# A graph network with a routed edge stage: the messages in two fp32r parts, a VectorE loop of twelve slots, and three columns of the routing marks on GpSimd

## The reference, cut to what matters

```python
x = x + gnn(layernorm(x), stack([src, dst]), edge_weight1, ...)
x = x + ffn(layernorm(x), ...)

def gnn(h, e, d2, ...):                 # 3125 nodes of 256, 103125 edges
    ei, ej = e[0], e[1]
    msg = silu(concat((h[ei], h[ej], d2)) @ mW1 + mb1)
    msg = layer_norm(msg, ln_g, ln_b)
    msg = silu(msg @ mW2 + mb2)
    agg = segment_sum(msg, ei, num_segments=3125)
    y = silu(concat((h, agg)) @ uW1 + ub1) @ uW2 + ub2
    return h + y
```

## Time and profile before

| | |
|---|---|
| time, median of 3 runs (lowest to highest) | 2228.12 us (2223.9 to 2229.85) |
| the profiled execution: time, span | 2226.9 us, 2225.2 us |
| busy share of the span | PE 88%, DVE 78%, ACT 59%, POOL 56% |
| mean granted TensorE clock | 0.946 |
| instruction packets (queues q8, q14) | 27 and 22 |

### The profile page before, as it was taken

The page is one execution under the profiler, slowest core; times in us unless marked ns, Lnnn a source line. Parts: engine busy times, 40 slices in busy tenths (PEclk is TensorE's granted clock), DMA queues, the critical chain, the costliest instruction groups (busy, mean ns, idle before and its releaser), DMA issues. The chain is left out here.

```text
span 2225.2 us, 45282 instructions
## 1 busy us (share of the span) xinstructions
PE 1961.5 (88%) x11037; PEld 1681.0 (76%) x11038; DVE 1736.7 (78%) x4578; ACT 1303.2 (59%) x2495; POOL 1238.9 (56%) x1177
## 2 busy tenths in 40 slices
PE   3546765379999999999999999999999999799996
PEld 2324554268888888888888888888888888677775
DVE  5899999678877877877878878778778778345895
ACT  1112331257777777777777777777777777423321
POOL 8753222376666666666667666666666665503000
PEclk9987777579999999999999999999999999899998
DMA  3000000344333333333333333333333333000001
GB/s 126 0 0 21 26 26 20 100 123 147 97 92 94 96 96 91 94 97 92 94 94 97 92 93 97 91 94 96 95 93 93 97 92 80 25 17 8 22 1 58
DMA packets 107787, 165.05 MB, mean 74 GB/s; under 512 B 42141, under 2 KB 78330, under 8 KB 107485
## 3 DMA queue, kind: packets, MB, share of 16 engines
q0 software_dynamic: 42016, 111.40, 18.4%
q1 hardware_dynamic: 59822, 47.94, 6.8%
q10 hardware_dynamic: 5900, 5.08, 0.7%
HBM read 152.30 MB, written 11.65 MB: 74 GB/s over the span
## 5 line engine op out<-in xcount | busy, mean ns | idle before, releaser
L907 POOL DMA_INDIRECT g_rows<-b_table,idx_ring x792 | 764.4, 965 | 439.7 <-ACT act L957 281.4
L1038 PE MATMUL ps<-w2g,nT 128*128 128x256 f32 x3336 | 789.3, 379 | 0.0
L1038 PEld LDWEIGHTS ps<-w2g,nT 128*128 128x128 f32 x3336 | 601.6, 190 | 64.6
L946 ACT ACTIVATE normed<-act,shift,rstd_e 128x255 f32<-128x255 f32 x834 | 449.6, 588 | 13.0 <-DVE shift L1105 9.5
L1021 PE MATMUL psG<-msg,ohf 128*125 128x256 f32 x1668 | 427.9, 379 | 0.1
L962 ACT ACTIVATE nT<-psM 128x512 f32<-128x512 f32 x417 | 248.9, 597 | 263.1 <-PE psM L1030 263.1
L1072 DVE TENSOR_TENSOR agg<-psG,agg 125x256 f32 x834 | 347.7, 417 | 67.6 <-issue 13.4
L1012 PE MATMUL psH<-a_sb,ohT 128*128 x1668 | 349.1, 332 | 26.4 <-DVE ohT L1125 24.7
L1136 DVE TENSOR_TENSOR g_rows<-psH,g_rows 128x512 f32<-128x512 f32 x417 | 284.7, 683 | 65.3 <-PE psH L1012 57.4
L1142 DVE BATCH_NORM_STATS2 stat_e<-act 128x6 f32<-128x256 f32 x834 | 310.2, 413 | 2.2 <-ACT act L957 2.2
L1021 PEld LDWEIGHTS psG<-msg,ohf 128*125 128x125 f32 x1668 | 284.4, 187 | 24.6 <-issue 0.3
(11 more groups left out here) (193 smaller groups left out, 1975.1 us busy)
## 6 DMA issues: line engine op xcount, KB each, us to landing
loc_rows<-loc_d SPq DMA_DIRECT2D x139, 187.5 KB
g_rows<-b_table,idx_ring POOLq DMA_INDIRECT x792, 2.8
h_sb<-in_x SPq DMA_DIRECT2D x1, 3125.0 KB
b_table<-b_out SPq DMA_DIRECT2D x25, 125.0 KB
x_all<-in_x ACTq DMA_DIRECT2D x1, 3125.0 KB
out<-x_all SPq DMA_DIRECT2D x5, 625.0 KB
ohT<-ew_d SPq DMA_DIRECT2D x139, 9.0 KB
idx_ring<-rec SPq DMA_DIRECT2D x132, 3.0 KB
```

Of the source, the lines that this page charges most:

```text
L907: pool.indirect_dma_start(g_rows[:, j, n, :], None, b_table[:, :], bass.IndirectOffsetOnAxis(ap=which, axis=0)).then_inc(s_gather[j], 16)
L946: ins = nc.scalar.activation(normed[:, j % 2, n, 0:D - 1], act1[:, (j - 10) % RING, n, 0:D - 1], ACT.Identity, scale=rstd_e[:, g % 2, k:k ...
L1038: mm = pe.matmul(ps2[:, k, n, :], nT[:, k, n, q, :], w2g[:, q, :], start=(q == 0), stop=(q == 1))
```

## The change

In the edge stage the float32 tile `msg` is replaced by two fp32r tiles. ScalarE writes Silu of ps2 to `high` (rounded to fp32r), and a second Silu, after `act1`, writes it back to ps2 in full precision. VectorE writes `low` = ps2 - `high`. `ohf` is fp32r too, and TensorE multiplies `ohf` with `high` and with `low` into the same psG. VectorE's loop runs 33 turns of 12 slots (SPAN = 2) with one load of 24 registers in each; the bodies that are written out keep 12. `shift` moves behind `ohf` in its slot. In routing VectorE writes marks for 10 of the 13 columns; GpSimd writes those of the other three (PCOLS), in a ring of four windows (PRING) that lies over f1 and f2, the first four windows before the `jump` chain and the others each behind a scatter.

```diff
+PCOLS = 3
+PRING = 4
+SPAN = 2
...
-            or_ = sb("or_", [P, 2, COLS, P], BF16)
+            or_ = sb("or_", [P, 2, COLS - PCOLS, P], BF16)
+            orp = [half[:, k * PCOLS * P // 2:(k + 1) * PCOLS * P // 2].bitcast(BF16).rearrange("p (t r) -> p t r", t=PCOLS)
+                   for half in (f1, f2) for k in range(PRING // 2)]
...
+                def pool_columns(s):
+                    if s >= PRING:
+                        pool.wait_ge(s_win, s - PRING + 1)
+                    for k in range(PCOLS):
+                        c = s * COLS + COLS - PCOLS + k
+                        ins = pool.tensor_scalar(orp[s % PRING][:, k, :], iota_n[:, :], r_all[:, c:c + 1], None,
+                                                 ALU.is_equal)
+                    ins.then_inc(s_orp, 1)
+
+                pool.wait_ge(s_places, 1)
+                for s in range(PRING):
+                    pool_columns(s)
                 pool.wait_ge(s_upto, 1)
...
                     pool.indirect_dma_start(rec_d[:, :], bass.IndirectOffsetOnAxis(ap=dest[:, s:s + 1], axis=0),
                                             recw[:, s % 4, :, :].rearrange("p w n -> p (w n)"), None).then_inc(s_scat, 16)
+                    if s + PRING < SUPERS:
+                        pool_columns(s + PRING)
...
                 def route(s):
                     pe.wait_ge(s_or, s + 1)
+                    pe.wait_ge(s_orp, s + 1)
...
-                        mm = pe.matmul(psK[:, s % 3, 0:PLANES * WIN], or_[:, s % 2, t, :],
+                        marks = or_[:, s % 2, t, :] if t < COLS - PCOLS else orp[s % PRING][:, t - COLS + PCOLS, :]
+                        mm = pe.matmul(psK[:, s % 3, 0:PLANES * WIN], marks,
...
-                    V.tensor_tensor(or_[:, s % 2, :, :], r_all[:, own].unsqueeze(2).broadcast_to([P, COLS, P]),
-                                    iota_v.unsqueeze(1).broadcast_to([P, COLS, P]), ALU.is_equal)
+                    mine = slice(s * COLS, (s + 1) * COLS - PCOLS)
+                    V.tensor_tensor(or_[:, s % 2, :, :],
+                                    r_all[:, mine].unsqueeze(2).broadcast_to([P, COLS - PCOLS, P]),
+                                    iota_v.unsqueeze(1).broadcast_to([P, COLS - PCOLS, P]), ALU.is_equal)
...
-            ohf = sb("ohf", [P, 2, 2, NB], F32)
+            ohf = sb("ohf", [P, 2, 2, NB], F32R)
-            msg = sb("msg", [P, 2, 2, D], F32)
+            high = sb("high", [P, 2, 2, D], F32R)
+            low = sb("low", [P, 2, 2, D], F32R)
...
-                        nc.scalar.activation(msg[:, (j - 13) % 2, :, :], ps2[:, (j - 13) % 2, :, :], ACT.Silu).then_inc(s_msg, 1)
+                        nc.scalar.activation(high[:, (j - 13) % 2, :, :], ps2[:, (j - 13) % 2, :, :], ACT.Silu).then_inc(s_high, 1)
                     if has(t, 4):
...
+                    if has(t, 13):
+                        act.wait_ge(s_high, t - 12)
+                        nc.scalar.activation(ps2[:, (j - 13) % 2, :, :], ps2[:, (j - 13) % 2, :, :], ACT.Silu).then_inc(s_msg, 1)
...
-                        pe.wait_ge(s_msg, t - 13)
+                        pe.wait_ge(s_low, t - 13)
...
-                            mm = pe.matmul(psG[0:NB, k, n, :], ohf[:, k, n, :], msg[:, k, n, :], start=True, stop=True)
+                            pe.matmul(psG[0:NB, k, n, :], ohf[:, k, n, :], high[:, k, n, :], start=True, stop=False)
+                            mm = pe.matmul(psG[0:NB, k, n, :], ohf[:, k, n, :], low[:, k, n, :], start=False, stop=True)
...
-                        need(pe, s_msg, t - 13)
+                        need(pe, s_low, t - 13)
...
-                regs = [dve.alloc_register(f"dve_block{n}") for n in range(2 * RING)]
+                regs = [dve.alloc_register(f"dve_block{n}") for n in range(SPAN * 2 * RING)]
...
-                    n0, n1 = 0, 2 * RING
+                    n0, n1 = 0, bodies * 2 * RING
...
-                    b = dve.snap(regs[2 * j + n], min_val=0, max_val=BLOCKS - 1)
+                    b = dve.snap(regs[2 * (i * RING + j) + n], min_val=0, max_val=BLOCKS - 1)
...
+                    if has(t, 13):
+                        dve.wait_ge(s_msg, t - 12)
+                        V.tensor_tensor(low[:, (j - 13) % 2, :, :], ps2[:, (j - 13) % 2, :, :], high[:, (j - 13) % 2, :, :],
+                                        ALU.subtract).then_inc(s_low, 1)
+
+                def bodies(d, count):
+                    prepare(d, count)
+                    for i in range(count):
+                        for j in range(RING):
+                            slot((d + i) * RING + j, d + i, j, i)
...
-                with dve.Fori(PEEL, DG) as d:
-                    body(d)
+                with dve.Fori(0, (DG - PEEL) // SPAN) as e:
+                    bodies(e * SPAN + PEEL, SPAN)
```

More of the change, by code:

```diff
@@ L42 @@
 MAGIC = 12582912.0
+assert (DG - PEEL) % SPAN == 0 and PAIRS % 3 == 0
 assert NODES == NB * BLOCKS and 0 < TAIL <= EC and (COLS * P + BLOCKS * (WIN - 1)) // WIN <= P
@@ L229, in build @@
             s_or = sem("s_or")
+            s_orp = sem("s_orp")
+            s_places = sem("s_places")
             s_win = sem("s_win")
@@ L707, in _ @@
                 link(V.tensor_scalar(r_all[:, :], f2[:, :], 1.0 / WIN, None, ALU.mult))
-                link(V.tensor_tensor(q_all[:, :], place[:, :], f2[:, :], ALU.subtract))
+                V.tensor_tensor(q_all[:, :], place[:, :], f2[:, :], ALU.subtract).then_inc(s_places, 1)
+                dve.wait_ge(s_places, 1)
                 def flat(ap):
@@ L837, in build @@
             s_second = sem("s_second")
+            s_high = sem("s_high")
             s_msg = sem("s_msg")
+            s_low = sem("s_low")
             s_ohf = sem("s_ohf")
@@ L1054, in _, with prepare @@
                 V = nc.vector
-                regs = [dve.alloc_register(f"dve_block{n}") for n in range(2 * RING)]
-                def prepare(d):
+                regs = [dve.alloc_register(f"dve_block{n}") for n in range(SPAN * 2 * RING)]
+                def prepare(d, bodies):
                     lo = d * 2 * RING - 2 * LAST
-                    n0, n1 = 0, 2 * RING
+                    n0, n1 = 0, bodies * 2 * RING
                     if isinstance(lo, int):
@@ L1064, in prepare, with add @@
                         dve.reg_load(regs[n0:n1], tile_block[0:1, bass.ds(lo + n0, n1 - n0)])
-                def add(t, j, n):
-                    b = dve.snap(regs[2 * j + n], min_val=0, max_val=BLOCKS - 1)
+                def add(t, j, i, n):
+                    b = dve.snap(regs[2 * (i * RING + j) + n], min_val=0, max_val=BLOCKS - 1)
                     room = agg[:, bass.ds(b, 1), :].rearrange("p a n -> p (a n)")
@@ L1106, in shifts, with slot @@
                                            op0=ALU.mult, op1=ALU.mult).then_inc(s_rstd, 1)
-                def slot(t, d, j):
+                def slot(t, d, j, i):
                     if isinstance(t, int) and t == LAST:
                         dve.wait_ge(s_clear, 1)
-                    shifts(t, d, j)
                     if has(t, LAST):
-                        add(t, j, 0)
+                        add(t, j, i, 0)
                     variance(t, d, j, 1)
@@ L1117, in slot @@
                     if has(t, LAST):
-                        add(t, j, 1)
+                        add(t, j, i, 1)
                     variance(t, d, j, 4)
@@ L1131, in slot @@
                                         ALU.is_equal).then_inc(s_ohf, 1)
+                    shifts(t, d, j)
                     if has(t, 2):
@@ L1144, in slot @@
                         ins.then_inc(s_bn, 1)
+                    if has(t, 13):
[7 more added lines that the diff above has]
+                            slot((d + i) * RING + j, d + i, j, i)
                 def body(d):
-                    prepare(d)
-                    for j in range(RING):
-                        slot(d * RING + j, d, j)
+                    bodies(d, 1)
                 V.tensor_copy(nodes, iota_n[:, 1:NB + 1]).then_inc(s_nodes, 1)
```

## The result

| | before | changed |
|---|---|---|
| median (lowest to highest), 4 runs each | 2227.01 us (2223.9 to 2229.85) | 2355.02 us (2354.26 to 2358.34) |
| ratio to before, 95% interval | | 1.0578 (1.056 to 1.0596) |
| span of the profiled execution | 2225.2 us | 2356.5 us |

The change makes the kernel slower by 128 us. The forecast was 2382 (155 more), with a range of 2280 to 2430. The direction, the place and the kind of loss were right; several terms were not.

What follows compares the result with a forecast made beforehand. TensorE was taken to bound the edge stage and VectorE the routing windows, with the edge stage's bound changing to VectorE. 2226.9 + 173 (edge loop) - 18 (routing) = 2382 us, range 2280 to 2430.

Steps and rivals of the forecast that it cites:

- two of the signs: Edge loop: granted clock below 1 and VectorE still waiting for psH were among the signs named for a wrong forecast.
- the interval of the forecast: Whole kernel: total of 2355 to 2410 us, with VectorE's load in proportion to its registers; chance 0.60.
- psG 0.67: Edge slot, TensorE: four fp32r matmuls take 0.67 us like psH, instead of 0.86; need falls 0.19 to 3.32 us.
- single passes: Edge slot, TensorE: the reading, rejected in the forecast, that psG's need falls by half of 0.86 us.
- The loop: +173 forecast: Edge loop: 66 turns of 21.03 us (1388) become 33 of 47.3 us (1561), so +173 us.
- the 47.3 us: VectorE's turn of 12 slots: 40.26, less one gap of 2.71, plus 7.20 for `low`, plus 2.73 for the load, less 0.2.
- The gap: I had 5.2: VectorE's loop start: stall left by the 24-register load (5.46 us), about 0.2 more of it covered by `low`.
- a rival at 12% with fetching: Edge loop: TensorE's clock falls in the load's gap, +33 to +66 us, or instructions are fetched each turn, +50 to +100; chance 0.12.
- proportion to the registers: VectorE's loop: a load of 24 registers takes twice the 2.73 us of 12, 5.46 us.
- the place of the first word to a rival: VectorE's load: slow only off a multiple of four words; gap nearly vanishes, total 2233 or 2207 us; chance 0.08.
- a slope: VectorE's load: 0.278 us a register from the rows of 6 and 12, giving an upper bound of 6.06 us for 24.
- Routing: -18 forecast: Routing windows: 24.8 us saved on VectorE's marks, less about 2 and 5 us lost; -18 us, bounds -25 and 0.

Runs made afterwards that it cites:

- e7_no_low: Changed kernel with six slots a turn and VectorE's load from word 12d - 32, `low` left out, `high` multiplied twice: 2055.47 us, ratio 0.9231.
- e3_routing_only: The kernel before with the routing half of the change alone, nothing of the edge stage: 2213.7 us, ratio 0.9939.
- e1_span1: The changed kernel with VectorE's loop at six slots a turn again (SPAN = 1): 2288.28 us, ratio 1.0276.
- e9_aligned12: The changed kernel with its twelve slots, VectorE's load moved to word 24e + 4 (28 registers): 2202.74 us, ratio 0.9897.
- e10_pcols2: The kernel before with the routing half alone and two marks columns on GpSimd instead of three: 2213.89 us, ratio 0.9944.
- e12_third: e8_half with two slots of six split in full, four for one tile, loop of six, `low` waiting for one semaphore: 2145.02 us, ratio 0.9639.
- e8_half: Changed kernel with six slots a turn and aligned load, only one tile of each pair split, the other in float32: 2166.36 us, ratio 0.9732.
- e2_loop_only: The kernel before with nothing but VectorE's loop of twelve slots and its load of 24 registers: 2327.9 us, ratio 1.0456.

## Why the prediction was right, and where it wasn't

**Right.** VectorE took the bound of the edge stage, by `low` (0.59 forecast 0.60) with nothing to hide it. The load of 24 registers was forecast as 5.46 and is 5.37 us. TensorE waits for ohT and `low`. Instruction packets are 27 and 24 (27 and 22 before), so nothing is fetched again. The routing window is 3.17 us. Not right: TensorE is busy 90% in the loop and not 84%, and two of the signs that I had named for being wrong came, a granted clock below 1 (0.94) and VectorE waiting for psH (24.6 us). The measured 2355 stands on the lower edge of the interval of the forecast (2355 to 2410): the loop was 31 us too dear, the routing gain 5 too large.

**The step that failed: psG 0.67.** I took the four fp32r matmuls at the price of psH, and wrote that TensorE's need falls "not by half of 0.86, as 'single passes' suggests". It does fall by nearly half, to 0.47 (e7_no_low); TensorE's need is 3.1 and not 3.32. The total survived by luck, because VectorE was above both. What the error hid is the chance in this change: had VectorE no more work, it would be worth 8%, routing and the moved load included. Why psH is dearer isn't shown; its matmuls differ from psG's in that their addresses come from registers, and that was not tried by itself.

**The loop: +173 forecast, +142 found** (33 x 46.36 = 1530 us against 1388; e3_routing_only gives +141). Per turn the 47.3 us split so:
- Twelve slots with `low`, without the gap: I took 12 x 3.50 = 42.0, worked out as a remainder of the turn. From `low` at 1202.58 to `low` at 1212.79 are three slots, 3.40 each: 1.2 us too much. The kernel before showed it, in the three slots behind its gap, where nothing waits (first additions at 1205.19 and 1213.66): (1213.66 - 1205.19) / 3 = 2.82, and with `low` 3.41.
- The gap: I had 5.2, it is 4.28, since a load is covered for 1.09 us and not for 0.2 to 0.5. The load starts 0.8 us before `low` does. 0.9 us too much.
- TensorE's clock: taken at nothing in the forecast, a rival at 12% with fetching. It shows: VectorE waits (24.6 us from 486 to 1875, about 0.8 a turn) for a psH that the half clock has made late. The rival's mechanism was real, and its size, by this wait, below the 1 to 2 us given. But the turns with 6.8 us at half clock are 1.2 us longer than those with 3.4, so the wait need not be all of it. In e1_span1, with a gap of 1.66 us, the clock stays at 1.00.
- Some 0.4 us a turn are left unexplained; whether they are the clock's too isn't shown.

**The reason for the load's price.** I took proportion to the registers and gave the place of the first word to a rival, with a chance of 0.08 and the remark that the new place 24e + 6 is off the multiple of four too. Both were true: the place is the cause, and off the multiple the price is proportional (12 in 2.73, 24 in 5.37, TensorE's 14 in 3.34; 0.22 to 0.24 us a register). That the forecast of 5.46 held with the wrong reason is luck: had the new loop's first word lain on the multiple, the time would have been near that of e9_aligned12 (2203 us). On it 16 take 1.11 and 28 take 1.85. The row of 6 registers in 1.06 us, from which I drew a slope, lay on it too (word 0; its 6 are no multiple of four), so it could not be compared with the 12 in 2.73, nor could TensorE's rows. The Trainium skill, page "Runtime: NRT & Kernel Launch", section "Instruction fetch mechanics", has some 200 ns a register also in bulk; the slow rows agree, the fast ones (0.06 a register between 16 and 28) don't, and the measurement decides.

**Routing: -18 forecast, -12.8 found** (the edge stage starts at 416.2 instead of 429.0; e3_routing_only -12.6). The window was right, and VectorE's last one ended 18.4 us earlier. But GpSimd's cycle of 3.06 us, forecast at 2.7, is too close to 3.17 for it to catch up on a delay. At 377.96 it has waited 7.65 us for a scatter to land, and the last one starts 11.3 us after VectorE's last marks instead of 6.0 before: 5.4 of the 18.4 are lost. With two columns these are 7.0 us, but VectorE's last marks come 3.9 later (e10_pcols2).

**Only argued:** that the clock costs 27 us in the changed kernel (0.8 x 33). The two kinds of turns support it (17 x 1.2 = 20 us between them), but no run kept TensorE busy through the gap.

## What to carry to other kernels

Price a register load by where its first word lies before its length, and look at what runs while it loads. Here about 1.1 us of a load was hidden behind `low` where it waits for one semaphore, 0.9 behind a short one (e12_third), and none where it waits for two (e8_half) or where the statistics stand last, as in the kernel before (a load of 2.73, gaps of 2.51 and 0.21) and in e7_no_low (1.10, 1.21). The number of waits is a likely cause, shown by one pair of kernels that differ in more than it, and it doesn't explain the statistics. Unrolling a loop to halve the number of loads doesn't halve the stall, since one load has one cover. A stall in one piece also costs more than in two, since the neighbours run dry (e2_loop_only, TensorE idle for 2.2 us a turn), and in the changed kernel TensorE is granted its lower clock as well. When a part moves from the bounding engine to one with little slack, move only so much of it as levels the two: in full it gave 2182 us, for one tile of two 2166, for two thirds 2145, though of these 21 us part is the shorter gap.

## What the runs showed of the hardware that was not expected

- TENSOR_LOAD of block numbers from SBUF: 12 registers 2.73 us, 24 registers 5.37 (VectorE, first word off a multiple of four words), 14 registers 3.34 (TensorE, off it); 12 registers 2.89 (TensorE, off it); 16 registers 1.10, 28 registers 1.85 (VectorE, on it), 12 registers 0.85 (TensorE, on it). On it, but with a number that is no multiple of four: 6 registers 1.06, 14 registers 1.32 (VectorE).
- An fp32r matmul of 256 columns with new weights follows the one before in 0.12 us (psG, e7_no_low); four of the psH group need 0.65.
- Idle for some 3 us and lightly used after it, TensorE was at 1.2 GHz for 3.4 or 6.8 us of a turn of 46 us; idle for 2.2 us (e2_loop_only), it fell in six turns only, for 3.4 us each.
